# Two gathers in place of one for six of seven tiles, in the last output stage of a graph network kernel

## What is computed

```python
def gat_layer(h, src, dst, W, al, ar, b):
    feat = (h @ W).reshape(n, H, F)                   # H = 4 heads, F = 64
    e = leaky_relu(el[src] + er[dst], 0.2)
    ex = exp(e - segment_max(e, dst)[dst])
    a = ex / segment_sum(ex, dst)[dst]
    out = segment_sum(feat[src] * a[:, :, None], dst) # sum over the edges of a node
    return elu(out + b).reshape(n, H * F)

h = relu(layernorm(x)); x = x + L0(h)
h = relu(layernorm(x)); x = x + gat_layer(gat_layer(h, ..1), ..2)
```

## Time and profile before

| | before |
|---|---|
| median of 3 runs | 7253.21 us (7250.66, 7253.21, 7256.73) |
| profiled execution: span of the core | 7256.0 us |
| DVE busy, whole span | 5474.7 us (75%) |
| POOL busy, whole span | 5227.7 us (72%) |
| PE, ACT busy, whole span | 2303.6 us (32%), 2204.3 us (30%) |
| DMA: mean of the span | 202 GB/s |
| last stage (from its first SP instruction to the end) | 7109.35 to 7256.0 us |

### The profile page before, as it was taken

One profiled execution on the slowest core, in us unless ns is written; L12 is line 12 of the kernel. 1 busy time (PEld: TensorE's weight loads), 2 busy tenths in 40 slices (PEclk: granted clock), 3 DMA queues, 4 the chain that ended last, 5 costly groups with the idle time before them and its releaser, 6 DMA issues. The chain is left out here.

```text
span 7256.0 us, 61622 instructions
## 1 busy us (share of the span) xinstructions
PE 2303.6 (32%) x10543; PEld 1546.4 (21%) x10543; DVE 5474.7 (75%) x9449; ACT 2204.3 (30%) x5437; POOL 5227.7 (72%) x5323
## 2 busy tenths in 40 slices
PE   4688888888888573000000000026000000000000
PEld 3455555555555462000000000014000000000000
DVE  7799999999999575666676767664566666666668
ACT  2688888888888341000000000001000000000001
POOL 4677777777776636777777777757777777777775
PEclk8899999999999797555555555568555555555555
DMA  7666676666666567676666666654567676766667
GB/s 227 189 203 204 204 205 204 204 204 203 204 204 188 139 164 186 208 221 211 218 213 215 216 213 218 210 155 102 179 209 223 208 223 208 221 210 219 212 211 237
DMA packets 822248, 1467.62 MB, mean 202 GB/s; under 512 B 216345, under 2 KB 552862, under 8 KB 821660
## 3 DMA queue, kind: packets, MB, share of 16 engines
q0 software_dynamic: 250192, 671.13, 34.7%
q1 hardware_dynamic: 571980, 795.64, 32.2%
HBM read 754.27 MB, written 713.36 MB: 202 GB/s over the span
## 5 line engine op out<-in xcount | busy, mean ns | idle before, releaser
L1774 POOL DMA_INDIRECT gb_g<-table,ix_g x3126 | 2976.1, 952 | 954.5 <-issue 949.2
L665 POOL DMA_INDIRECT gb<-table,ix x1563 | 1615.9, 1034 | 494.9 <-issue 471.6
L1855 DVE SCALAR_TENSOR_TENSOR gb_g<-gb_g,same_g,wv 128x256 f32<-128x256 f32 x3028 | 1452.1, 480 | 93.6
L1050 PE MATMUL pm<-ident,tl 128*4 128x128 f32 x2 | 0.7, 372 | 4035.4 <-DMA tl<-sums 4035.4
L1787 ACT ACTIVATE ww<-ee 128x132 f32<-128x132 f32 x98 | 27.8, 284 | 3643.1 <-DVE ee L1832 3643.1
L1843 DVE TENSOR_TENSOR wv<-gb_g,ww 128x1024 f32<-128x1024 f32 (+1 forms) x782 | 954.8, 1221 | 0.0
L696 PE MATMUL po<-msg,sel 128*128 128x256 f32 x3144 | 858.1, 420 | 148.2 <-DVE msg L808 143.9
L1823 DVE TENSOR_TENSOR ee<-gb_g,held 128x128 f32<-128x128 f32 (+1 forms) x98 | 37.4, 381 | 1110.1 <-DMA gb_g<-table,ix_g 1110.1
L1050 PEld LDWEIGHTS pm<-ident,tl 128*4 128x4 f32 x2 | 0.2, 81 | 4036.2 <-DMA tl<-sums 4036.2
L696 PEld LDWEIGHTS po<-msg,sel 128*128 128x128 f32 x3144 | 614.1, 206 | 384.0 <-DVE msg L808 237.3
L688 PE MATMUL pt<-m,r 64*128 64x256 f32 x3136 | 461.9, 412 | 228.0 <-DVE msg L849 225.5
(11 more groups left out here) (282 smaller groups left out, 4326.2 us busy)
## 6 DMA issues: line engine op xcount, KB each, us to landing
sums<-gb_g SPq DMA_DIRECT2D x780, 528.0 KB, 3.5
sums<-ost SPq DMA_DIRECT2D x393, 512.0 KB, 3.2
gb_g<-table,ix_g POOLq DMA_INDIRECT x3126, 3.1
gb<-table,ix POOLq DMA_INDIRECT x1563
table<-f SPq DMA_DIRECT2D x48, 520.0 KB, 6.8
x<-in_x SPq DMA_DIRECT2D x50, 256.0 KB, 3.9
at<-in_rbf SPq DMA_DIRECT2D x100, 128.0 KB
hT_d<-hT SPq DMA_DIRECT2D x49, 256.0 KB, 3.4
```

The costliest lines, as they stand in the source:

```text
L665: eng.indirect_dma_start(out=gb[:, g, j, :, :].rearrange("p a c -> p (a c)"), out_offset=None, in_=q.table0[:, :], in_offset=bass.Indirect ...
L1774: eng.indirect_dma_start(out=gb[:, p, j, 0:FR], out_offset=None, in_=q.table1[:, :], in_offset=bass.IndirectOffsetOnAxis(ap=ix[:, p, j:j + ...
L1855: ins = eng.scalar_tensor_tensor(rows[:, t, 0:D], behind, same[:, t:t + 1], wv[k % 2][:, j, :], ALU.mult, ALU.add)
```

## The change

For n = 2, tile t is gathered in two pieces whose first has `FIRST_ROWS[t % 7]` partitions and whose second has the rest; where the entry is 128 there is one piece, as before. [...] What DVE waits for counts the pieces. The stage for n = 1 keeps one gather for each tile.

```diff
+FIRST_ROWS = (P, 64, 109, 124, 122, 120, 96)
...
+        pieces = lambda t: 1 + (FIRST_ROWS[t % len(FIRST_ROWS)] < P)
         moved = lambda g, m: 16 * sum(size(y) for y in range(g % m, g + 1, m))
+        gathered = lambda g: 16 * sum(pieces(t) if n == 2 else 1 for y in range(g % B, g + 1, B) for t in tiles_of(y))
...
+            rest = {r: sb(c, f"rest{r}", [P - r, NT], I32) for r in FIRST_ROWS if r < P}
+            s_rest = q.sem(f"o{n}_rest")
...
+                    for r, x in rest.items():
+                        eng.dma_start(x[:, :], q.row_idx[r:P, 0:NT]).then_inc(s_rest, 16)
                     for g in range(B):
                         eng.dma_start(x1[g][:, 0:size(g), :], nodes(q.x1_d, g)).then_inc(s_x1[g], 16)
...
                     for i, t in enumerate(tiles_of(g)):
-                        eng.indirect_dma_start(out=rows[g % B][:, i, :], out_offset=None, in_=q.sums1_x,
-                                               in_offset=col(q.row_idx, t)).then_inc(s_row[g % B], 16)
+                        r = FIRST_ROWS[t % len(FIRST_ROWS)] if n == 2 else P
+                        eng.indirect_dma_start(out=rows[g % B][0:r, i, :], out_offset=None, in_=q.sums1_x,
+                                               in_offset=col(q.row_idx[0:r, :], t)).then_inc(s_row[g % B], 16)
+                        if r < P:
+                            eng.indirect_dma_start(out=rows[g % B][r:P, i, :], out_offset=None, in_=q.sums1_x,
+                                                   in_offset=col(rest[r], t)).then_inc(s_row[g % B], 16)
...
+                if n == 2:
+                    eng.wait_ge(s_rest, 16 * len(rest))
                 for g in range(3):
                     gather(g)
...
-                    eng.wait_ge(s_row[g % B], moved(g, B))
+                    eng.wait_ge(s_row[g % B], gathered(g))
```

## The result

The changed kernel takes 7385.4 us (median of 4 runs, 7379.8 to 7386.7), the one before 7251.9 us in the same session (4 runs, 7247.9 to 7256.7): 1.018 times as long, 95% interval 1.0167 to 1.0193, or 133 us more. The forecast was 7337 with a range of 7301 to 7400; the time lies inside the range, 48 us above the point, and 7 us from rival 2.

What follows compares the result with a forecast made beforehand. DVE bounds the last stage now, POOL would after the split: 90.7 us more POOL work plus 3.9 late start less 11.5 slack gives +83 us, 7337 us off the median; range 7301 to 7400.

Steps and rivals of the forecast that it cites:

- rival 2: POOL's gathers: uneven pieces cost by rows per DMA engine, the largest divisor up to 16; +139 us, 7392, chance 0.26.
- the forecast's own case: Last stage: each piece costs POOL 786 ns plus 1.25 ns a row; +83 us, 7337, chance 0.52.
- rival 1: POOL's gathers: every piece costs a full gather, 946 ns however short; +97 us, 7351, chance 0.08.
- the low bound: POOL's gathers: a fixed part of 362 ns, taken from the scatters' 4.6 ns a row; +48 us, 7301.
- POOL becomes the bound, by the number of gathers: Last stage: 182 gathers for 98 take POOL 8.7 us per group, above DVE's 5.36, so DVE waits in each group.
- What one piece costs: POOL's gathers: 786 ns plus 1.25 ns a row, so a tile's two pieces take 1732 ns where one took 946.
- rival 3: POOL's gathers: a piece costs in proportion to its rows, only 84 gaps are added; +17.6 us, 7271, chance 0.06.
- Rival 4: Last stage: DVE stays the bound and hides the added pieces; only the late start shows, +3.9 us, 7257, chance 0.03.
- The late start: Stage start: POOL's first gather waits for six small index copies issued by SP, 3.9 us late.
- The slack: Stage end: POOL's last rows land 11.5 us before DVE's last reciprocal, which absorbs that much of POOL's added time.
- The transfers at no cost: Last stage's DMAs: the same bytes spread over some 90 us more, costed at nothing; DMA share falls to about 0.6.
- Theory A: From the experiments, POOL's gathers: 0.86 us plus 13.3 ns per row on one engine, using the largest divisor up to 16.

Runs made afterwards that it cites:

- the probe: The kernel before plus, behind its end, gathers of sixteen lengths, wide and narrow rows, then sets of eight without waits; 127 wide rows took POOL 2.57 us.
- the copies alone: Against the changed kernel, all tiles keep single 128-row gathers while the six index copies and POOL's wait stay; 0.9992 times the kernel before.
- b_mult16: Against the changed kernel, first pieces of 128, 64, 112, 112, 112, 112 and 96 rows, still 182 gathers; 1.0079 times the kernel before.
- b_after: The changed kernel, unchanged, rerun on another chip in the same session as the kernel before; 1.0129 times the kernel before.

## Why the prediction was right, and where it was off

The direction, and POOL as the new bound, came out as forecast. That the time lies inside the range owes something to luck: the forecast's own case and rival 1 end at 7351, and the range reached 7400 only to take in rival 2. By its own sign the prediction's price was wrong: it was to be so "if pieces of odd counts differ from those of 64, 96 and 32 by more than their rows explain", and 109 rows took 2.30 us where 64 took 0.90. (The other sign held narrowly: POOL's first gather started 5.51 us after SP's first instruction, which is 7114.86 by the clock of the trace before. The sum itself gives 7253.21 + 83.1 = 7336.3, where 7337 was written, and the low bound's 362 ns is the gather's 946 less 128 x 4.56, while the scatters' own two figures leave 432; neither matters to what follows.)

- *POOL becomes the bound, by the number of gathers.* Right. 182 gathers were issued, and POOL's gaps stayed at 0.30 us. DVE waits in 22 of 25 groups. That each wait would be about 3 us was wrong: reciprocals mostly follow in turn at 13 to 15 us and at 5.4 to 7, 144.4 us of waits in all and not 80. Why the groups come in pairs is open; with multiples of 16 they do so too. The 80 did not fit the forecast's own sum either, which adds 83 us to the 15.1 of before.
- *What one piece costs.* This is the step that failed, a term of the sum that was mis-sized: "By that slope a gather costs 786 ns whatever its rows, plus 1.25 ns for each". The fixed part is 860 ns, and the rest goes by the rows of the fullest DMA engine, 13 ns each. The sum was 158.7 us busy and measured 203.4, 44.7 more. By the probe's figures: 182 x (0.860 - 0.786) = 13.5 from the fixed part, and the other 31.2 from the rows. The fullest engines' rows in a round come to 255 (8 for 128; 4 + 4; 109 + 19; 31 + 1; 61 + 1; 8 + 1; 6 + 2), times 14 rounds and 13.3 ns 47.5 us, where I had 15.7 (the two parts come out 0.6 us above the measured sum).
- *Why the slope misled.* The 112 rows and the 128 in the earlier trace rows are seven and eight rows for each of 16 engines, one step of 13 ns apart. I read 20 ns, and carried it back over eight steps to find the fixed part: an error of 7 ns became one of 56, most of the 74 that were missing.
- *Rival 2.* Its mechanism was right in every piece, and its two sizes were off in opposite ways (786 and 20 ns in place of 860 and 13). Its 214.5 us busy was 11 too many, since 13.5 us too few in the fixed part and some 24 too many in the rows partly cancel; that its 7392 came within 7 us is in part luck. I gave it 0.26 because no row had a count that 16 does not divide. That was a fair account of the rows, but the evidence for my own form, that the price goes by rows whatever divides them, was no better: the same two sizes fit both.
- *Rivals 1 and 3.* A full price for each piece (0.946) and a price in proportion to the rows both fall; 2 rows take 0.87 us.
- *Rival 4, hidden.* It needed 90 ns for an added piece; they add 0.86 us and more, and a gap of 0.30.
- *The late start.* Forecast 3.9 us, measured 4.8, shown by the copies alone. The copies issued at 0.69 us each (543 to 732 ns, with a gap), above my 0.43 to 0.61. It is paid in full.
- *The slack.* Forecast 11.5 us, measured 10.1 (POOL's end to the kernel's end, 23.7 to 13.6). The missing part is at the end: the last group did not wait for its rows, the one before did, until 7370.42, while its piece of 122 rows, 61 for one engine, had started at 7363.68. The probe has 6.34 us from start to landing for 61 wide rows on one engine (1.67 + 4.68). This is the "up to 3 us" that the prediction gave to a hot engine, there for the 109 rows; some 2 us by this account. `b_mult16`, which has no such piece, agrees: from POOL's end to the last reciprocal it has 2.0 us, `b_after` 4.35. No run isolates it, and the lag of other groups in `b_mult16` varies by more (1.3 to 4.9 us).
- *The transfers at no cost.* Right: the DMA share fell from 0.95 to 0.57 (forecast 0.6).

Together, against the forecast of +83 and the measured +131 in the stage: 44.7 for the pieces, 0.9 for the start, 1.4 for the slack, and the rest, about 1, in the gaps.

## What to carry to other kernels

A gather issued by POOL costs about 0.86 us before its first row and 0.30 us of gap, so splitting one in two adds 1.17 us of POOL even when no row is added: merge gathers. Do not count on another engine's being the bound to hide a split: with 8 of 98 tiles split under a lead of some 10 us, the stage still grew by 10.3 us. Choose row counts that 16 divides; if a tile has an odd remainder, gather the next multiple of 16, since 112 rows cost POOL 0.92 to 0.94 us and land 1.92 us after that, where 109 cost 2.30 and land 6.81 us after it. And where two sizes in a trace fit two laws, ask what else differs between them before extending either: a short probe of sixteen lengths settled in one run what the profile could not.

## What the runs showed of the hardware that was not expected

- POOL's time for a gather does not depend on the bytes of a row: 127 rows took 2.57 us with 1056 bytes each and 2.56 with 16. Eight such gathers ran back to back at 2.55 to 2.56 us, with none of them held up, and had all landed 31.5 us after the first start, where their rows on one single engine would need 53 us by the estimate of 52 ns a row.
- 127 rows of 1056 bytes took 10.06 us from start to landing, where 128 rows took 3.02. By Theory A the first are on one DMA engine and the others on sixteen; 127 against 109 rows give 52 ns for a row, or 20 GB/s.
- The stage bound by POOL had the same length to 0.1 us on two chips (277.7 and 277.8 us) that differ by 20% for the whole kernel before (7252 and 8682 us).
